# Attention operands of iteration 0 allocated outside the attention block, cleared earlier and staged during the projection

## Time and profile before

| | us |
|---|---|
| median of 3 runs | 2281.39 (2277.24 to 2284.3) |
| the profiled execution, its time | 2276.35 |
| the profiled execution, its span | 2274.3 |
| PE busy in the span | 2078.4 (91%) |
| DVE busy | 1601.7 (70%) |
| ACT busy | 1353.0 (59%) |
| POOL busy | 497.1 (22%) |

### The profile page before, as it was taken

How to read it: one execution, slowest core, us unless ns; L and a number is a source line. 1 busy time by engine, 2 the same in 40 slices (tenths; PEclk the granted TensorE clock), 3 DMA queues, 4 the chain that set the end, 5 groups by cost and what they waited for, 6 DMA issues and landing times. The chain is left out here.

```text
span 2274.3 us, 45896 instructions
## 1 busy us (share of the span) xinstructions
PE 2078.4 (91%) x17861; PEld 1302.5 (57%) x17861; DVE 1601.7 (70%) x2067; ACT 1353.0 (59%) x2612; POOL 497.1 (22%) x550
## 2 busy tenths in 40 slices
PE   4998779999999999979969998849999999988998
PEld 3887633333333333358858887725555555547888
DVE  7776489999999999566764447847776777726333
ACT  3444238888888888824434445507776767652454
POOL 3000142111231321330012113952212212111110
PEclk9999869999999999999989999959999999989999
DMA  4003752243353452220030001882454446310000
GB/s 140 1 0 131 259 81 48 44 78 71 79 92 62 92 97 49 55 65 1 0 118 1 1 0 53 269 147 51 86 105 84 95 87 112 64 50 19 28 18 28
DMA packets 124668, 162.76 MB, mean 72 GB/s; under 512 B 54456, under 2 KB 77752, under 8 KB 124472
## 3 DMA queue, kind: packets, MB, share of 16 engines
q1 hardware_dynamic: 108168, 122.29, 25.1%
q0 software_dynamic: 15488, 36.22, 6.0%
q10 hardware_dynamic: 816, 1.57, 0.2%
HBM read 95.04 MB, written 63.70 MB: 70 GB/s over the span
## 5 line engine op out<-in xcount | busy, mean ns | idle before, releaser
L1477 DVE TENSOR_REDUCE att_maxes<-att_s_max 128x2 f32<-128x1024 f32 (+2 forms) x832 | 974.1, 1183 | 187.1 <-PE att_s_max L1298 88.3
L1456 ACT ACTIVATE att_probs<-att_s_exp 128x512 f32<-128x512 f32 (+3 forms) x1792 | 887.9, 552 | 241.9 <-PE att_s_exp L1298 112.0
L1379 PE MATMUL att_o_ps<-att_probs,att_v_st 128*32 128x256 f32 (+1 forms) x6912 | 527.2, 377 | 15.1 <-ACT att_o_sb L1435 14.4
L1355 PE MATMUL att_s_exp<-att_q_st,att_k_st 64*128 64x512 f32 (+3 forms) x1792 | 459.2, 475 | 4.4 <-ACT att_probs L1456 3.9
L1315 PE MATMUL att_s_max<-att_k_st,att_q_st 62*128 62x512 f32 (+3 forms) x1792 | 394.2, 417 | 67.8 <-DMA att_k_st<-k_parts 52.3
L1355 PEld LDWEIGHTS att_s_exp<-att_q_st,att_k_st 64*128 64x128 f32 x1792 | 189.8, 184 | 344.0 <-ACT att_probs L1456 296.5
L1379 PEld LDWEIGHTS att_o_ps<-att_probs,att_v_st 128*32 128x32 f32 x6912 | 138.3, 108 | 255.2 <-issue 139.4
L1315 PEld LDWEIGHTS att_s_max<-att_k_st,att_q_st 62*128 62x128 f32 x1792 | 189.4, 194 | 91.3 <-issue 55.4
L1550 POOL TENSOR_TENSOR att_m_parts<-att_m_turned,att_zeros 32x128 fp32r<-32x128 f32 x64 | 28.9, 451 | 529.6 <-ACT att_m_turned L1422 388.9
L588 DVE TENSOR_TENSOR ffn1b_h_lo<-ffn1b_h,ffn1b_h_hi 128x512 fp32r<-128x512 f32 x64 | 44.5, 696 | 112.5 <-PE ffn1b_acc L135 94.2
L1563 POOL DMA_DIRECT2D attention_rows<-att_o_sb x64 | 37.5, 586 | 358.8 <-ACT att_o_sb L1435 355.1
(11 more groups left out here) (310 smaller groups left out, 3919.1 us busy)
## 6 DMA issues: line engine op xcount, KB each, us to landing
att_q_st<-q_parts SPq DMA_DIRECT2D x384, 64.0 KB, 5.3
att_k_st<-k_parts SPq DMA_DIRECT2D x192, 128.0 KB, 4.9
attention_rows<-att_o_sb POOLq DMA_DIRECT2D x64, 256.0 KB, 3.6
output_wide<-attention_weights POOLq DMA_DIRECT2D x36, 256.0 KB, 5.7
q_parts<-qkv_parts SPq DMA_DIRECT2D x16, 512.0 KB, 3.8
k_parts<-qkv_parts SPq DMA_DIRECT2D x16, 512.0 KB, 2.7
v_rows<-qkv_vt SPq DMA_DIRECT2D x16, 512.0 KB, 4.1
att_v_raw<-v_rows SPq DMA_DIRECT2D x32, 256.0 KB, 5.5
```

The lines of the kernel that those rows point to most:

```text
L1355: mm = pe.matmul(s_exp[:, plan.bank[place], q0:512], k_st[rows, it.set, pr, kt * P:(kt + 1) * P], q_st[rows, it.set, qc, pr, q0:512], star ...
L1379: mm = pe.matmul(o_ps[j * VW:(j + 1) * VW, cols], v_st[:, it.par, kt, j, :], probs[:, step % 2, j, cols], start=kt == 0 and part == 0, sto ...
L1456: act.activation(probs[:, step % 2, j, q0:512], s_exp[:, plan.bank[place], q0:512], ACT.Exp, scale=1.0 if causal else 0.25).then_inc(s["ex ...
L1477: v.tensor_reduce(maxes[:, qc, :, pairs, qt - 4 * qc, kc], banks, AX.X, ALU.max).then_inc(s["max_done"], 1)
```

## The change

- The tiles of set 0 of `q_st` and `k_st`, and `ones`, are allocated for the whole layer instead of in the attention block. POOL clears them whole (`clear_operands`): in layer 0 at the beginning of load0, in layer 1 at the end of its program in ffn1a.
- The rows of ones of set 0 and the 18 staging DMAs of iteration 0 move to the projection. In qkv0 POOL issues them, after a wait for the stores of the first two chunks, and waits for their landing at its end. In qkv1 SP issues them behind the stores of chunk 2, and waits for them at its end.
- In the attention block the ones of sets 1 and 2 are 4 DMAs instead of 2 for all three, and staging of set 2 goes behind `put_max(0, 0)` and `put_max(0, 1)`. PE's waits for pads, staging and ones follow.
- The swapped mask tables of layer 1 shrink from 2048 to 128 columns, and the path for masks that aren't outweighed uses one matmul per mask instead of two.

```diff
@@ load_stage, gpsimd
+            if integer:
+                clear_operands(p, E)
@@ ffn_stage, gpsimd
             if not gated:
                 each_chunk(p, body)
+                if follow:
+                    clear_operands(p, E)
@@ qkv_stage
+        @block.gpsimd
+        def _(p):
+            put_ones(p, E, 0, s["ones_early"])
+            for made in range(KC):
+                p.wait_ge(parts_out[made], 16 * QK)
+            stage_operands(p, E, It(0, 0), s["staged_early"], s["staged_early"])
+            p.wait_ge(s["staged_early"], 16 * (STAGE_FIRST + STAGE_SECOND))
+            p.wait_ge(s["ones_early"], 2 * 16)
@@ rope_stage, sync
+            for number in range(E.early):
+                put_ones(sp, E, number, E.st_sem["ones_in"])
             for c in range(CHUNKS):
...
+                if KC <= c < KC + E.early:
+                    for made in range(KC):
+                        sp.wait_ge(parts_out[made], 16 * QK * PARTS)
+                    stage_operands(sp, E, It(0, c - KC))
+            for number in range(E.early):
+                sp.wait_ge(E.st_sem[f"staged{number}"], 16 * STAGE_FIRST)
+                sp.wait_ge(E.st_sem[f"staged_second{number}"], 16 * STAGE_SECOND)
+            sp.wait_ge(E.st_sem["ones_in"], 2 * 16 * E.early)
@@ new functions
+def clear_operands(p, E):
+    p.memset(E.ones[:, :], 1.0).then_inc(E.st_sem["ones_set"], 1)
+    for number in range(E.early):
+        for i, tile in enumerate((E.q_st[number], E.k_st[number])):
+            p.memset(tile[:, :, :].bitcast(F32), 0.0).then_inc(E.st_sem["pads"], 1)
+            p.wait_ge(E.st_sem["pads"], 2 * number + i + 1)
+
+def put_ones(sp, E, number, landed):
+    sp.wait_ge(E.st_sem["ones_set"], 1)
+    if number < E.early:
+        sp.wait_ge(E.st_sem["pads"], pads_done(E, number + 1))
+    for slot in range(2):
+        dst = E.k_st[number][(slot + 1) * HALF - MROWS:(slot + 1) * HALF, :, :].rearrange("o b (c n) -> o (b c) n", n=P)
+        sp.dma_start(dst.bitcast(F32), E.ones[:, :].unsqueeze(1).to_broadcast([MROWS, PAIRS * (S // P), P])).then_inc(landed, 16)
@@ attention_stage, sync
-            sp.wait_ge(s["ones_set"], 1)
...
+            for number in range(E.early, SETS):
+                put_ones(sp, E, number, E.st_sem["ones_in"])
...
-                stage(start)
                 stage_v(start)
-                stage(start.ahead(1))
+                stage_operands(sp, E, start.ahead(1))
                 stage_v(start.ahead(1))
-                stage(start.ahead(2))
                 put_max(start, 0)
 
                 def body(it, first, last):
                     left = ITERS - 1 - it.r if isinstance(it.k, int) else SETS
                     put_max(it, 1)
-                    if left >= 2 and not first:
-                        sp.wait_ge(s["st_ready"], plan.pieces(it, 0, 0))
-                        stage(it.ahead(2))
+                    if left >= 2:
+                        if not first:
+                            sp.wait_ge(s["st_ready"], plan.pieces(it, 0, 0))
+                        stage_operands(sp, E, it.ahead(2))
@@ attention_stage, gpsimd
-            p.memset(ones[:, :], 1.0).then_inc(s["ones_set"], 1)
-            clear_pads(0)
...
-            for number in range(1, SETS):
-                clear_pads(number)
+            for number in range(max(E.early, 1), SETS):
+                clear_pads(p, E, number)
@@ program
+            alloc_operands(nc, E, layer, "operands0", 1, 1)
+            alloc_operands(nc, E, layer, "operands1", 1, 0)
```

More of the change, by code:

```diff
@@ new lines, in put_ones, with stage_operands @@
+def put_ones(sp, E, number, landed):
+    sp.wait_ge(E.st_sem["ones_set"], 1)
+    if number < E.early:
+        sp.wait_ge(E.st_sem["pads"], pads_done(E, number + 1))
+    for slot in range(2):
+        dst = E.k_st[number][(slot + 1) * HALF - MROWS:(slot + 1) * HALF, :, :].rearrange("o b (c n) -> o (b c) n", n=P)
+        sp.dma_start(dst.bitcast(F32), E.ones[:, :].unsqueeze(1).to_broadcast([MROWS, PAIRS * (S // P), P])).then_inc(landed, 16)
+def stage_operands(sp, E, it, first=None, second=None):
+    heads = slice(it.hg * GH * HD, (it.hg + 1) * GH * HD)
+    for qc in range(KC):
+        landed = (second or E.st_sem[f"staged_second{it.set}"]) if qc else (first or E.st_sem[f"staged{it.set}"])
+        for slot in range(2):
+            for g, (pq, pk) in enumerate(zip(PARTS_Q, PARTS_K)):
+                rows = slice(slot * HALF + PAD + g * HD, slot * HALF + PAD + (g + 1) * HD)
+                src = E.q_dram[pq, heads, it.b * S + qc * 512:it.b * S + (qc + 1) * 512]
+                sp.dma_start(E.q_st[it.set][rows, qc, :, :].bitcast(F32),
+                             src.rearrange("(pr s d) n -> s d pr n", d=HD, s=2)[slot]).then_inc(landed, 16)
+                if qc == 0:
+                    src = E.k_dram[pk, heads, it.b * S:(it.b + 1) * S]
+                    sp.dma_start(E.k_st[it.set][rows, :, :].bitcast(F32),
+                                 src.rearrange("(pr s d) n -> s d pr n", d=HD, s=2)[slot]).then_inc(landed, 16)
@@ L1314, in max_unit @@
                             rows = slice(slot * HALF, (slot + 1) * HALF - MROWS)
-                            mm = pe.matmul(s_max[:, a % MBUFS, slot, begin:begin + keys], q_st[rows, it.set, qc, pr, (qt - 4 * qc) * P:(qt - 4 * qc + 1) * P],
-                                           k_st[rows, it.set, pr, kc * 512:kc * 512 + keys], start=True, stop=not masked)
+                            mm = pe.matmul(s_max[:, a % MBUFS, slot, begin:begin + keys], q_st[it.set][rows, qc, pr, (qt - 4 * qc) * P:(qt - 4 * qc + 1) * P],
+                                           k_st[it.set][rows, pr, kc * 512:kc * 512 + keys], start=True, stop=not masked)
                         if masked:
@@ L1354, in scores @@
                     rows = slice(slot * HALF, (slot + 1) * HALF)
-                    mm = pe.matmul(s_exp[:, plan.bank[place], q0:512], k_st[rows, it.set, pr, kt * P:(kt + 1) * P],
-                                   q_st[rows, it.set, qc, pr, q0:512], start=True, stop=not masked)
+                    mm = pe.matmul(s_exp[:, plan.bank[place], q0:512], k_st[it.set][rows, pr, kt * P:(kt + 1) * P],
+                                   q_st[it.set][rows, qc, pr, q0:512], start=True, stop=not masked)
                     if masked:
@@ L1518, in _ @@
         def _(p):
-            p.memset(ones[:, :], 1.0).then_inc(s["ones_set"], 1)
-            def clear_pads(number):
-                for i, tile in enumerate((q_st, k_st)):
-                    for slot in range(2):
-                        rows = tile[slot * HALF:slot * HALF + PAD, number, :, :]
-                        p.memset(rows.bitcast(F32), 0.0).then_inc(s["pads"], 1)
-                        p.wait_ge(s["pads"], 4 * number + 2 * i + slot + 1)
-            clear_pads(0)
             for n, (tile, value) in enumerate(fills):
```

78 lines of the change are left out of this document (39 added, 39 removed).

## The result

The changed kernel took 2250.45 us (median of 4 runs, 2248.63 to 2254.65) against 2279.35 for the kernel before; the ratio is 0.9873, 95% interval 0.9849 to 0.9896. Run again beside other kernels it took 2247.84 us, ratio 0.9865, interval 0.9848 to 0.9881. The forecast was 2256.0, range 2248 to 2270.

What follows compares the result with a forecast made beforehand. Attention openings, where every engine waits for iteration 0's staging DMAs, were taken as the bound. att0 14.4 - 1.0 and att1 15.4 - 3.4 give 25.4 us, so 2281.39 - 25.4 = 2256.0 us, range 2248 to 2270.

Steps and rivals of the forecast that it cites:

- The openings: Starts of att0 and att1: PE no longer waits for iteration 0's staging, gaining 14.4 and 15.4 us.
- First unit: Attention openings: PE's first max unit comes 0.15 us after att0's begin and 0.55 us after att1's.
- unchanged pace: Attention openings: max units and reductions run as fast as before, 29.0 us to first scores in att0, 27.8 in att1.
- POOL's split: att1's opening: POOL finishes splitting the maxima, after its pad clears, 19.4 us into the block.
- the maxima without a wait: att1's opening: maxima issued by 22.1 us, scores due at 28.4, so the earlier 0.56 us wait goes.
- qkv0: Layer 0's projection: staging by POOL costs 1.0 us, bounds 0 and 11.5, with 12.1 us of DMA time free.
- the set's price: DMA engine time for staging one set, taken from att0's opening: at most 11.5 us.
- slack of 6 us: qkv0: chunk 2's last k store has 6 us to spare, after a 3 us landing, before ACT rewrites its buffer.
- the rival of slow issue: qkv0: POOL needs much longer per DMA beside DVE work; at 6 us each about 2310 us; chance 3%.
- qkv1: Layer 1's projection: 11.5 us of staging by SP against 8.1 free delays the end by 3.4 us; bounds 0 and 9.4.
- one of 6 us: qkv1: ACT stands about 6 us for chunk 3's stores queued behind the staging, partly hidden, not charged separately.
- ACT waiting several times: Either projection: ACT and PE waiting several times for stores would show the prediction wrong.

Runs made afterwards that it cites:

- Clears only: Changed kernel with nothing staged in the projections; both attention blocks stage iteration 0 themselves again: 2273.43 us, ratio 0.9973.
- set 2 ahead of the maxima: Changed kernel with the third set of operands staged before the first maxima in both attention blocks, as before the change: 2252.70 us, ratio 0.9879.
- two sets: Changed kernel with POOL staging the operands of iterations 0 and 1 in layer 0's projection, instead of iteration 0 only: 2255.79 us, ratio 0.9895.
- layer 1 only: Changed kernel with the change kept in layer 1 and layer 0 put back as in the kernel before: 2265.07 us, ratio 0.9936.
- qkv0 by SP: Changed kernel with layer 0's projection staging issued by SP behind chunk 2's stores instead of by POOL: 2251.35 us, ratio 0.9876.
- fetch experiment: Changed kernel with POOL's fetch of finished outputs in att0 begun only after the next iteration's first-half maxima have landed: 2248.02 us, ratio 0.9860.
- best kernel: Changed kernel with att0's output fetch behind the maxima and the second half of iteration 0's queries staged in att1 instead of qkv1: 2244.23 us, ratio 0.9849.
- spread staging: Changed kernel with qkv1's 18 staging DMAs issued three at a time behind the stores of chunks 2 to 7: 2250.86 us, ratio 0.9883.
- last experiment: The best kernel with unread PE matmuls added at qkv1's end and behind every max unit of both opening lists: 2263.33 us, ratio 0.9946.

## Why the prediction was right, step by step

- *The openings* (14.4 and 15.4 us) came out at 14.4 and 15.5. First unit, unchanged pace, POOL's split at 19.9 us into att1's block for 19.4 forecast, the maxima without a wait: as told. Clears only and set 2 ahead of the maxima each put one part back and find its wait.
- *qkv0* (1.0 us) was -0.06. The term that was too large is the set's price, 11.5 us from att0's opening; beside the stores it is 6.6. I took 1.0 because free time is never filled whole; with two sets the share reached 0.99. That it came out at nothing is in part luck: I counted the slack of 6 us behind a landing of 3, the stores beside the staging took 8.8, and 0.4 us of the slack was left. POOL's issue was 0.50 us instead of 0.80, with DVE busy 34.39 of the 54.9 us, so the rival of slow issue never came near.
- *qkv1* (3.4 us) was 1.77; over all traces it is 97.6 to 99.1 us with the whole set staged against 95.9 to 96.8 without, some 2 us. The size came near, the way was another, and that much is luck. The 3.4 us were transfers left over at the end of the stage. With 8.2 us for the set and 8.1 free there are hardly any, and from DVE's last write to the next block it is 7.85 us for 7.71. The delay came through ACT, whose wait the prediction told and then counted as nothing of its own: I forecast one of 6 us, there were two, 5.1 and 4.2, and 1.63 us of them reached the last write. Counting the backlog once was right, but it was paid in the middle of the stage and not at its end. ACT waiting several times was on the list of what would show the prediction wrong, and for this term it did.
- *Missed: a wait in att0.* The prediction counted nothing behind the openings. Three times, when a new sequence begins, the maxima land behind POOL's fetch of outputs, 1.7 us of waiting in this trace. The seven traces with POOL's staging in qkv0 and the old place of the fetch have these waits; the kernel before, clears only, layer 1 only and qkv0 by SP have none; moving the fetch removes them. That the two compete is shown. How DMAs that ended long before make the maxima land later is open. POOL issues 20 there, 18 of the staging and 2 of ones, and no run parts these. The packets show this much: in the four traces without the waits the last of the maxima's packets of 512 bytes starts 7.0 to 7.5 us behind the fetch's issue, in the seven with them 8.1 to 8.8, while in the change the fetch itself takes no longer than before (8.6 to 8.9 us for 8.7 to 9.0).
- *Missed: the clock behind att1's first scores.* The prediction moved everything behind a first unit by one amount. The shift of 24.53 at the first scores is 22.76 at the first store. Windows of the first 9 us behind the first scores, before and then after:

```profile
1531.50:1534.50 3.00, 2.94 (x21) 2.05 (x21) 1.60 (x2) 1.41 (x3) 2.26 (x1) 0.50 0.03 7
1534.50:1537.50 3.00, 3.00 (x38) 1.71 (x36) 2.12 (x4) 2.50 (x6) 0.00 (x0) 0.89 0.38 86
1537.50:1540.50 3.00, 3.00 (x49) 1.84 (x49) 2.57 (x3) 1.46 (x6) 0.00 (x0) 1.00 0.02 5
```

```profile
1507.00:1510.00 3.00, 3.00 (x27) 2.11 (x22) 2.29 (x3) 1.46 (x3) 3.00 (x2) 0.50 0.02 4
1510.00:1513.00 3.00, 3.00 (x28) 1.76 (x26) 1.49 (x3) 1.58 (x4) 0.02 (x1) 0.50 0.73 150
1513.00:1516.00 3.00, 3.00 (x31) 1.16 (x29) 1.75 (x2) 1.67 (x5) 0.00 (x0) 0.71 1.08 131
```

PE is busy throughout in both, and its clock (third column from the end) is at 0.50 for one more window after the change. In the change run again, in layer 1 alone and in the fetch experiment it was up in the second window (0.91, 0.96 and 0.96), so this belongs to the execution more than to the change.

The terms add up to 28.2 us (14.4 + 0.06 + 15.5 - 1.77) against 25.4 forecast. The start of qkv0, att0's waits, out0 and ffn1a (0.25 + 1.78 + 1.28 + 0.48) take some back, ffn0b gives 0.11, and behind att1's first scores the execution gained 2.2: 26.7. Out0 has a granted clock of 0.91 after and 0.95 before, out1 0.99 and 0.97: the blocks do the same work, and their lengths go the way of the clock.

## What to carry to other kernels

Where a block opens with a DMA that every engine waits for, moving it into the block ahead is worth nearly the whole wait, as long as the DMA engines there have idle time of the transfer's size; read this from the DMA share of that stretch. Have the moved transfers issued by an engine that has nothing else to issue there that others wait for, read how much slack is left to the transfers that they delay, and then look for small urgent DMAs later that are issued together with a large one. A wait that appears in the trace isn't yet a price: here 9.3 us of waiting cost 1.6, 6.0 us in qkv1 of the best kernel cost nothing, and three short waits that nobody looked for cost 1.8. What a wait cost is read from the last work of the stage, with and without it. And an experiment that takes a wait away can move the end of the stage itself, as the spread staging did.

## What the runs showed of the hardware

- The same 18 transfers have no one price. They cost at most 11.5 us of engine time among themselves (att0's opening before), 6.6 from POOL beside qkv0's stores, 8.2 from SP beside qkv1's, and some 12 from SP in qkv0 (a share of 0.79 of 85.76 us against 0.68 of 81.34 before).
- A busy PE isn't a fast one: 32.00 of 32.00 us busy at 0.50, mostly with 62-row matmuls and behind a pause of 3.87 us, while matmuls of 128x512 at the end of the block ahead ran at 1.00. Why is not settled.
- Executions of one kernel differ by up to 13 us (2260.47 to 2273.9 in the last experiment), and the profiled ones show a stretch of low clock late in att1 that comes and goes, where ACT and PE do the same work. Windows of it in the fetch experiment and in the kernel before:

```profile
1974.00:1992.00 18.00, 17.15 (x137) 6.72 (x129) 0.00 (x0) 11.06 (x27) 7.15 (x6) 0.56 0.19 61
```

```profile
2011.00:2023.00 12.00, 10.98 (x84) 3.76 (x83) 0.00 (x0) 9.11 (x18) 2.94 (x2) 0.72 0.15 48
```

In the changed kernel's own trace it is missing. A gain of 2 us in one block is better judged by that block's length in the trace than by the median.
